# Where the softmax mask is laid down: one matmul moved and padded, and the last tile's end on other engines

## The reference

```python
x = x + L0(x, cond_512, ...)   # keys = modulated linear of x; 16 x 16 attention between the heads, inside
                               # token pairs; softmax; then a modulated output projection
x = x + L1(x, cond_512, ...)   # low-rank weight decoded from the condition
x = x + L2(x, cond_512, ...)   # modulated linear, clipped to +-256
x = x + L3(x, ...)             # layer norms with gathered gains, h = silu(cat @ W1 + b1) @ W2 + b2,
                               # and at its end the layer norm below
def _ln(x, g, b):
    m = jnp.mean(x, axis=-1, keepdims=True)
    v = jnp.mean((x - m) ** 2, axis=-1, keepdims=True)
    return (x - m) * jax.lax.rsqrt(v + EPS) * g + b
```

## Time and profile before

| | us |
|---|---|
| runs of the kernel before | 1055.29, 1057.75, 1057.88 (median 1057.75) |
| the profiled execution, its own time | 1056.21 |
| its span, first to last instruction | 1054.3 |
| PE busy | 996.6 (95% of the span) |
| DVE busy | 664.7 (63%) |
| ACT busy | 486.1 (46%) |
| POOL busy | 703.6 (67%) |
| mean granted PE clock, share of full | 0.985 |

### The profile page before, as it was taken

The page is one execution under the profiler, slowest core; times in us unless marked ns, Lnnn a source line. Parts: engine busy times, 40 slices in busy tenths (PEclk is TensorE's granted clock), DMA queues, the critical chain, the costliest instruction groups (busy, mean ns, idle before and its releaser), DMA issues.

```text
span 1054.3 us, 18130 instructions
## 1 busy us (share of the span) xinstructions
PE 996.6 (95%) x6546; PEld 780.5 (74%) x6546; DVE 664.7 (63%) x1210; ACT 486.1 (46%) x763; POOL 703.6 (67%) x635
## 2 busy tenths in 40 slices
PE   6989999999999796999999999999999999999993
PEld 3566777767777475888888887888888888888882
DVE  5677777678768767657557558556556556555441
ACT  2678768775767534334334335324324324323321
POOL 4556665667665348758768768767767767777852
PEclk9989999999999998999999999999999999999997
DMA  9634653544322554232232234233223233132310
GB/s 265 220 118 136 210 212 142 197 167 138 131 88 62 154 178 138 70 104 92 75 115 97 73 111 142 72 95 120 69 92 124 65 101 120 62 108 77 103 42 20
DMA packets 56156, 124.04 MB, mean 118 GB/s; under 512 B 7827, under 2 KB 10005, under 8 KB 55044
## 3 DMA queue, kind: packets, MB, share of 16 engines
q1 hardware_dynamic: 44292, 80.94, 22.9%
q0 software_dynamic: 11776, 41.95, 12.9%
HBM read 104.91 MB, written 17.95 MB: 117 GB/s over the span
## 4 chain that ended last, share of the span: by engine, by line
PE 76%; DVE 7%; issue 6%; POOL 5%; ACT 3%; DMA 1%; SPq 0%; POOLq 0%; DVEq 0%; ACTq 0%
PE ps L597 39%; PE ps_y L604 7%; PE ps_k L669 6%; PE ps_o L604 5%; PE tp L609 5%; PE ps_v L658 2%; PE tp L897 2%; PE ps_s L645 1%; PE ps L976 1%; PE ps_u L690 1%; POOL kb L1669 1%; POOL e L1663 1%; PE ps_z L885 1%; DVE xl L1313 1%; ACT k_diag L993 1%
## 5 line engine op out<-in xcount | busy, mean ns | idle before, releaser
L1715 POOL TENSOR_TENSOR rstd<-var_eps,half 128x1 f32<-128x1 f32 x96 | 54.7, 570 | 118.5 <-DVE var_eps L1510 117.7
L1647 POOL TENSOR_TENSOR om<-om,bc 128x512 f32<-128x512 f32 x32 | 48.1, 1504 | 82.6 <-DVE om L1319 82.6
L1184 ACT ACTIVATE g_out<-ps 128x512 f32<-128x512 f32 x32 | 19.1, 598 | 178.0 <-PE ps L976 178.0
L993 ACT ACTIVATE at_diag<-at 32x512 f32<-32x512 f32 x128 | 80.2, 626 | 7.8 <-DVE at L1293 6.7
L1516 DVE TENSOR_SCALAR shift_n<-mean_var,rstd 128x1 f32<-128x1 f32 x96 | 20.5, 214 | 97.1 <-POOL rstd L1715 95.1
L993 ACT ACTIVATE k_diag<-kt 32x512 f32<-32x512 f32 x128 | 80.1, 625 | 1.1
L1496 DVE TENSOR_TENSOR t_lo<-tp,t_hi 128x512 fp32r<-128x512 f32 x64 | 43.8, 684 | 31.3 <-ACT t_hi L1121 31.3
L1125 ACT ACTIVATE h<-h,shift_n,rstd 128x512 f32<-128x512 f32 x32 | 26.1, 816 | 80.1 <-DVE shift_n L1516 80.1
L1659 POOL TENSOR_SCALAR xb<-xb,bias_o 128x512 f32<-128x512 f32 x32 | 52.2, 1633 | 11.3 <-DMA xb<-in_x_wide 11.2
L1663 POOL TENSOR_TENSOR e<-e,rinv 128x512 f32<-128x512 f32 x32 | 33.6, 1051 | 36.4 <-DVE rinv L1280 36.4
L669 PE MATMUL ps_k<-wk_hi,xh 128*128 128x512 f32 x128 | 55.8, 436 | 0.2 <-DVE xl L1313 0.2
(11 more groups left out here) (286 smaller groups left out, 3240.6 us busy)
## 6 DMA issues: line engine op xcount, KB each, us to landing
raw<-in_dec_w SPq DMA_DIRECT2D x30, 512.0 KB, 6.1
x_in<-in_x_turned SPq DMA_DIRECT2D x32, 256.0 KB, 5.3
xb<-in_x_wide SPq DMA_DIRECT2D x32, 256.0 KB, 4.0
x_dram<-xb SPq DMA_DIRECT2D x32, 256.0 KB, 3.4
xt<-x_dram SPq DMA_DIRECT2D x8, 1024.0 KB, 8.3
out<-o SPq DMA_DIRECT2D x32, 256.0 KB, 2.0
raw<-in_int_W SPq DMA_DIRECT2D x7, 1024.0 KB, 6.6
wk_raw<-in_w_k_t SPq DMA_DIRECT2D x4, 256.0 KB, 6.3
```

Of the source, the lines that this page charges most:

```text
L993: last = nc.scalar.activation(dst[g, :, q, :], src[g, :, :], ACT.Copy)
L1647: nc.gpsimd.tensor_tensor(om[:, :], om[:, :], bc[:, STYLE_O, t // TB, :], ALU.mult).then_inc(mix_step, 1)
L1715: nc.gpsimd.tensor_tensor(rstd[:, k:k + 1], var_eps[:, k:k + 1], half[:, :], ALU.pow).then_inc(norm_step[k], 1)
```

## The change

PE issues the mask of the next tile at the end of the output projection, one step early, ahead of the L690 product and of the L701 transposes. With it goes the wait for "low". The two operands become 128 rows high, with zeros below the two rows that count. For the last tile alone, POOL's three operations of LN3 are replaced: reciprocal on DVE and square root on ACT for the power, and DVE for the two 512-wide operations.

```diff
 # PE, attend, tile s-2
                     if later(t, 1):
                         pe.wait_ge(v_ready, t)
-                    else:
-                        pe.wait_ge(mask_ready, 2)
-                        pe.wait_ge(diag_zero, 3)
...
                     pe.wait_ge(k_diag_ready, t + 1)
-                    if later(t, 1):
-                        pe.wait_ge(softmax_step, nth(SOFTMAX, "low", t))
-                    nc.tensor.matmul(ps_s[:, :, :], mask_lr[:, :], mask_rr[:, :], start=True, stop=False, skip_group_check=True)
...
                     product_turned(ps_o, ...).then_inc(o_done, 1)
+                if has(1):
+                    if later(s, 2):
+                        pe.wait_ge(softmax_step, nth(SOFTMAX, "low", s - 1))
+                    else:
+                        pe.wait_ge(mask_ready, 2)
+                        pe.wait_ge(diag_zero, 3)
+                    nc.tensor.matmul(ps_s[:, :, :], mask_lr[:, :], mask_rr[:, :], start=True, stop=False, skip_group_check=True)
 # ACT, refine
                     high("s", c, tp[1], l3_done, c)
+                if d == T - 1:
+                    act.wait_ge(norm_step[LN3], nth(NORM, "var", T) + 1)
+                    nc.scalar.activation(rstd[:, LN3:LN3 + 1], inverse[:, :], ACT.Sqrt).then_inc(norm_step[LN3], 1)
 # DVE, prepare(-1): the copies write rows 0:2 of the padded operands
-                    nc.vector.tensor_copy(mask_lr[:, :], ...)
+                    nc.vector.tensor_copy(mask_lr[0:2, :], ...)
 # DVE, refine, after the last tile's shift
+                if f == T - 1:
+                    dve.wait_ge(fn_ready, T)
+                    dve.wait_ge(tables_in, 16 * 3)
+                    nc.vector.tensor_tensor(f2[:, :], f2[:, :], gain[:, :], ALU.mult).then_inc(fg_ready, 1)
+                    dve.wait_ge(fg_ready, T)
+                    dve.wait_ge(stored, 16 * f)
+                    nc.vector.tensor_tensor(o[:, :], f2[:, :], x3s[f % 4][:, :], ALU.add).then_inc(o_ready, 1)
 # DVE, refine, after the last tile's var_eps
+                if d == T - 1:
+                    dve.wait_ge(norm_step[LN3], nth(NORM, "var", T))
+                    nc.vector.reciprocal(inverse[:, :], var_eps[:, LN3:LN3 + 1]).then_inc(norm_step[LN3], 1)
 # POOL, first instructions; and the last tile left out of its LN3 operations
+            nc.gpsimd.memset(mask_lr[:, :].bitcast(F32), 0.0)
+            nc.gpsimd.memset(mask_rr[:, :].bitcast(F32), 0.0)
-                if has(2):
+                if has(2) and f < T - 1:
...
-                if has(1):
+                if has(1) and d < T - 1:
                     power(LN3, d)
 # buffers
-            A["mask_rr"] = sb1("mask_rr", [2, F], F32R)
-            A["mask_lr"] = sb1("mask_lr", [2, P], F32R)
+            A["mask_rr"] = sb1("mask_rr", [P, F], F32R)
+            A["mask_lr"] = sb1("mask_lr", [P, P], F32R)
```

More of the change, by code:

```diff
@@ L214, in body @@
         M[n] for n in ("out_raw", "a_stage", "b2", "gain", "shift", "id_rows", "one_hot", "pid"))
-    stats, mean_var, var_eps, rstd, shift_n = (M[n] for n in ("stats", "mean_var", "var_eps", "rstd", "shift_n"))
+    stats, mean_var, var_eps, inverse, rstd, shift_n = (M[n] for n in ("stats", "mean_var", "var_eps", "inverse", "rstd", "shift_n"))
     hi, lo = M["hi"], M["lo"]
@@ L1123, in normalize @@
             def normalize(k, t, dst, src):
-                act.wait_ge(norm_step[k], nth(NORM, "shift", t + 1))
+                act.wait_ge(norm_step[k], nth(NORM, "shift", t + 1) + (k == LN3 and t == T - 1))
                 nc.scalar.activation(dst, src, ACT.Identity, bias=shift_n[:, k:k + 1], scale=rstd[:, k:k + 1]).then_inc(applied[k], 1)
@@ L1350, in prepare @@
                     dve.wait_ge(consts_in, 16 * 4)
-                    nc.vector.tensor_copy(mask_lr[:, :], at[0:2, 0:4, :].rearrange("p a b -> p (a b)")).then_inc(mask_ready, 1)
-                    nc.vector.tensor_copy(mask_rr[:, :], e[0:2, :, :].rearrange("p a b -> p (a b)")).then_inc(mask_ready, 1)
+                    nc.vector.tensor_copy(mask_lr[0:2, :], at[0:2, 0:4, :].rearrange("p a b -> p (a b)")).then_inc(mask_ready, 1)
+                    nc.vector.tensor_copy(mask_rr[0:2, :], e[0:2, :, :].rearrange("p a b -> p (a b)")).then_inc(mask_ready, 1)
                     dve.wait_ge(squares_step, 3)
@@ L1512, in shifts @@
             def shifts(k, t):
-                dve.wait_ge(norm_step[k], nth(NORM, "rstd", t + 1))
+                dve.wait_ge(norm_step[k], nth(NORM, "rstd", t + 1) + (k == LN3 and t == T - 1))
                 if later(t, 1):
@@ L1802, in program @@
             A[n] = sb(n, shape)
-        for n, shape in (("half", [P, 1]), ("stats", [P, 3, 6]), ("mean_var", [P, 3, 2]), ("var_eps", [P, 3]), ("rstd", [P, 3]), ("shift_n", [P, 3])):
+        for n, shape in (("half", [P, 1]), ("stats", [P, 3, 6]), ("mean_var", [P, 3, 2]), ("var_eps", [P, 3]), ("inverse", [P, 1]), ("rstd", [P, 3]), ("shift_n", [P, 3])):
             M[n] = sb(n, shape)
```

## The result

| | us |
|---|---|
| kernel after, median of 5 runs | 1049.12 (1046.9 to 1049.68) |
| kernel before, on the same chip, median of 5 | 1057.75 (1055.04 to 1060.2) |
| ratio, 95% interval | 0.9928 (0.9905 to 0.9951) |
| profiled execution, its own time and span | 1049.68 and 1047.9 (before: 1056.21 and 1054.3) |

The change saves 0.7% by the ratio (7.6 us, interval 5.2 to 10.0), 8.6 us between the medians. The forecast was 1053.8 us with a range down to 1050.4: the sign was right, and the size was outside the range.

What follows compares the result with a forecast made beforehand. PE was three quarters of the chain, nearly neck and neck with DVE in the first half. Mask 1.3 plus last tile 1.4 saved 2.7 us, giving 1053.5, set up to 1053.8; range 1050.4 to 1057.0.

Steps and rivals of the forecast that it cites:

- The last tile: Last tile's norm: moving POOL's three operations to DVE and ACT saves about 1.4 us, all on the path.
- the sum: Whole kernel: 1.3 us from the mask plus 1.4 from the last tile, 2.7 us saved.
- five cases: Whole kernel: forecast (0.45), DVE closing gaps (0.17), whole PE saving (0.22), slower (0.09), exposed table load (0.07).
- the rival at 1050.4: Whole kernel: PE's full 5.0 us arrives plus 1.4 from the tail, 6.4 us less; chance 0.22.
- The mask, what goes and what comes: PE's list per tile: 0.96 us goes, 0.53 and 0.23 come, so 0.20 us saved.
- The mask, where it counts and what it takes back: First-half chain: nine masks save 1.8 us, two delayed transposes lose 0.46, net 1.3 us.
- The whole saving: Steps 8 to 32: all 25 x 0.20 = 5.0 us of PE's saving arrives; time 1050.4; chance 0.22.
- DVE closes every gap: Attention steps: the mask brings 0 and only the tail's 1.4 us stays; time 1055.4; chance 0.17.
- The slower rival: L701 transposes 0.23 us later in 25 steps cost 5.8 us, 4.4 slower net; time 1061.2; chance 0.09.
- The last tile's own chain: Last tile, `var_eps` start to `o` end: 4.55 us shrinks by 1.47 to 3.1.
- The base of the sum: Starting time: profiled 1056.21 gives 1053.5, set up to 1053.8 because the four times average 1056.8.
- The table load: Last tile's square root: 1.28 us load hides in ACT's idle time; exposed, tail saves 0.1, time 1055.1, chance 0.07.

Runs made afterwards that it cites:

- e3: Kernel after plus one useless one-column POOL memset that waits for the last tile's `o`; 1054.75 us, 0.9967 of the kernel before.
- e6: Kernel before plus one extra POOL drain behind the last gathers, in the last step but two; 1050.37 us, 0.9943 of the kernel before.
- e5: Kernel after with only the last tile's power back on POOL, the two wide operations still on DVE; 1053.4 us, 0.9959 of the kernel before.
- e7: Kernel after with the padded mask behind the L702 transposes instead of ahead of them and the decoder product; 1048.29 us, 0.9916 of the kernel before.
- e10: The kernel of e7 run again, beside e9, e11 and e12 on one chip; 1048.14 us, 0.9908 of the kernel before.
- e9: The kernel after, unchanged, run again beside e10, e11 and e12 on one chip; 1045.98 us, 0.9903 of the kernel before.
- e11: The kernel of e1 run again, beside e9, e10 and e12 on one chip; 1050.49 us, 0.9935 of the kernel before.
- the two-row version: Kernel after with the moved mask's operands two rows high again, without the two memsets; 1050.07 us, 0.9931 of the kernel before.
- e8: Kernel before with POOL's table-row gathers replaced by memsets to one, so it computes something else; 1047.99 us in a single execution.
- e2: Kernel after with the last tile's three operations given back to POOL, leaving the mask change alone; 1055.59 us, 0.9977 of the kernel before.
- e1: Kernel before with the last tile's edits alone, mask as before; 1050.11 us, 0.9928 of the kernel before.
- e12: Kernel after with the mask padded but in its old place between key transposes and scores; 1049.65 us, 0.9915 of the kernel before.

## Why the prediction was wrong

*The step that failed* is "The last tile", and by it the sum. It ended at `o` and took what lies behind it, 9.7 us from 1044.64 to the span's end, as fixed. The term that is missing is POOL's drain at the end of the block: 5.7 us. Taking POOL's last three operations away does not only shorten their chain; it lets POOL begin to drain 8.8 us earlier (1034.5 against 1043.3). The runs show in its place: one memset behind `o` puts the end of POOL's drain 5.9 us behind SP's again (e3), one early drain gives 6.0 us (e6), and with POOL's last operation in between the drain ends 3.1 us behind SP's (e5). With the term, the working gives 2.7 + 5.7 = 8.4 us, inside the measured interval of 5.2 to 10.0.

It could have been read before. The chain that ended last in the kernel before closes with this row (start, us, what):

```profile
1043.35 1.30 POOLq L236
```

It names POOL's queue at the line that closes the block, not a computation, and the end of the span is another 9.7 us away. The prediction looked at the chain up to `o` and never asked which engine comes last behind it. None of the five cases contained the term either: the rival at 1050.4 came near the result with a reason that is false (PE's whole saving of 5.0 us arriving).

*The mask, what goes and what comes*: right. 0.21 us in PE's list against 0.20, pitch by pitch.

*The mask, where it counts and what it takes back*: right in mechanism. The chain masks arrive whole, the plain steps not at all. Of the two losses of 0.23 the one at 132.38 came; at 234.61 none is seen, since e7 and e10 have the same steps there as the kernel after. That is 0.9 us in the 15 steps. Up to 331.8 us e9 has gained 1.67 and e10 1.86 us on the kernel before since 94 us (e11, tail alone, 0.05), against a forecast of 1.3 net. The whole saving is refuted: 15 x 0.20 would be 3.0 in that stretch. So is "DVE closes every gap". The slower rival has a real mechanism (0.23 us in one step, and the two-row version lost 1.0), but far from its price of 5.8.

*The last tile's own chain*: right, 4.55 - 3.13 = 1.42 us against 1.47.

*The base of the sum*: 2.7 us were taken off 1056.5, while the rivals start from 1056.8, so their times and the forecast are 0.3 us apart by that alone. It decides nothing.

*The table load*: right. It ran at once behind ACT's last copy and was hidden. The changed tail does not test what an exposed switch costs, but the kernel before has one, where the load stands behind a wait:

```profile
431.06 1.28 ACT L1184 ACT_TABLE_LOAD   x1 [2.40 <-DVE wout_low L1492]
432.36 0.60 ACT L1184 ACTIVATE g_out<-ps 128x512 f32<-128x512 f32 x1
```

From the load's start to its operation's start it is 1.30 us. The Trainium skill puts a switch at about 2.66 us with a drain ("ScalarE: Activation LUTs", What ACT_TABLE_LOAD costs). The trace shows no such drain, and the measured 1.30 us decides.

*The ledger of the two profiled executions* (the kernel after against before, us): at 279 us it is 2.9 ahead, of which 1.8 were there at the first value mixing (44.81 against 46.59; e8 and e11, with the mask as before, start it at 44.80 too) and 1.1 came since; from 279 to 302 it loses 2.8; from 302 to 401 it wins 1.2; to 1034.5 it loses 0.4; the last tile's last product loses 1.6, the chain behind it wins 1.4. That is 0.7 at the end of `o`, and 5.7 behind it. The loss at 279 to 302 is PE's clock and not the change: e9, the same program, took 22.54 us for these two steps at a clock of 1.00, the kernel after 25.69 and the kernel before 22.92. The loss in the last product is not the change either, and the gain at 364 to 376 goes with the clock, as the last section shows.

## What to carry to other kernels

Read the program's end as a stage of its own: for every engine, when its last operation ends, when its drain ends, and which of them the closing meeting waits for. Once POOL has issued gathers, it should have drained since, or have no work in the last 6 us before the last result is done (an estimate: 7.9 us of drain less the 2.2 from the end of `o` to SP's drain); that was worth 5.7 us here, twice the 2.7 that the forecast found in the computation. On PE, order matmuls so that the shape of the array changes seldom: padding a two-row operand with zeros to the shape of its neighbours saved 0.2 us a tile in PE's list, of which the steps on the chain kept all and the others nothing. Padding it in its old place would have done as well as moving it.

## What the runs showed of the hardware that was not expected

POOL's drain lasts until 7.9 us behind its last operation when it has issued gathers since its last drain (9228 to 9252 ns in ten executions whose last operation is the wide one of 1.3 us; 8515 and 8030 behind shorter ones), and ends with that operation otherwise (1362 and 1364 ns). It does not depend, over what these runs cover, on how long ago the last gather was issued. In the kernel before that was at 999.5 us and no gather packet moved after 1005 us; POOL's last operation ends at 1044.64 there, at 1035.80 in the kernel after and at 1044.05 in e3, and the drain ends 7.9 to 8.0 us behind it each time. In e6 it is 8.0 us too, with the operation's end at 1023.78, some 21 us behind the last gather's issue.

PE's granted clock falls at different places in executions of one and the same program. The stretch of 286 to 294 us (length, busy PE, PEld, DVE, ACT and POOL with counts, granted clock, DMA share, GB/s) in the kernel after:

```profile
286.00:294.00 8.00, 8.00 (x87) 6.85 (x87) 3.92 (x7) 3.27 (x7) 3.81 (x3) 0.58 0.29 101
```

and in e9, which is the same kernel:

```profile
286.00:294.00 8.00, 8.00 (x93) 6.67 (x94) 4.28 (x8) 5.48 (x9) 5.49 (x5) 1.00 0.19 64
```

The first is mostly at the lower level of 1.2 GHz, the second at 2.4 throughout, and so is the kernel before (1.00). From 364 to 376 us it is the kernel before that has less, 0.72, against 0.86 after and 1.00 in e9. What PE did ahead of the fall at 287 us in the kernel after is a run of products with two columns:

```profile
284.79 1.05 PE L624 MATMUL ps_x<-pick,u_row 128*128 128x2 f32 x8
285.77 1.05 PE L839 MATMUL ps_x<-last_u,v_rows 32*128 32x2 f32 x8
286.75 1.39 PE L841 MATMUL ps_x<-last_m,r_rows 64*128 64x2 f32 x8
```

e9 has the same run and did not fall, so it is not enough by itself. The twelve matmuls of the last product took 4.63 us in the kernel after and 3.03 in the kernel before; both values come up in kernels with and without the mask's edit (3.0 in e2 and e9 with it and in e1 without, 4.6 in the kernel after and e12 with it and in e11 without). Single executions of e9 run from 1043.21 to 1051.0 us, which is as much as the whole effect of the change. Why the clock falls in one execution and not in the next stays open.
